# Attention kernel on one core: the product of probabilities and values over 512 queries at once, with five buffers for transposed heads

## What is computed

```
scores = jnp.einsum('bnhd,bmhd->bhnm', q, k) * scale        # 8 heads, HD = 32
scores = jnp.where(mask, jnp.float32(-jnp.inf), scores)
attn = jax.nn.softmax(scores, axis=-1)
h = jnp.einsum('bhnm,bmhd->bnhd', attn, v).reshape(b, n, d)  # the product of the change
h = h @ Wo + bo                                              # then residual and layer norm
```

## Time and profile before

| | |
|---|---|
| median of 3 runs | 1259.42 us (1255.37 to 1261.86) |
| span of the profiled execution | 1260.3 us, its own time; nothing is added around it in what follows |
| TensorE busy | 1175.5 us, 93% |
| VectorE busy | 1044.5 us, 83% |
| ScalarE busy | 881.5 us, 70% |
| one loop body | 73.88 us, 14 of them |
| granted TensorE clock, mean | 0.989 |

### The profile page before, as it was taken

The page is one execution under the profiler, slowest core; times in us unless marked ns, Lnnn a source line. Parts: engine busy times, 40 slices in busy tenths (PEclk is TensorE's granted clock), DMA queues, the critical chain, the costliest instruction groups (busy, mean ns, idle before and its releaser), DMA issues.

```text
span 1260.3 us, 28368 instructions
## 1 busy us (share of the span) xinstructions
PE 1175.5 (93%) x9440; PEld 846.5 (67%) x9440; DVE 1044.5 (83%) x2767; ACT 881.5 (70%) x2024; POOL 489.0 (39%) x337
## 2 busy tenths in 40 slices
PE   5877999999999999999999999999999999999896
PEld 2744767677776767767676776767677676767564
DVE  4775888889788888979889897988979798897686
ACT  3245786777777677777767777776777768677674
POOL 1360235433443443345334433633443363333320
PEclk9998999999999999999999999999999999999999
DMA  8125172543526153362624436153343615333321
GB/s 253 48 51 134 44 183 54 130 113 87 132 52 195 41 137 99 85 151 51 168 69 106 119 85 163 52 153 83 101 118 85 167 52 155 81 85 85 84 68 34
DMA packets 182208, 130.84 MB, mean 104 GB/s; under 512 B 108464, under 2 KB 161712, under 8 KB 182064
## 3 DMA queue, kind: packets, MB, share of 16 engines
q1 hardware_dynamic: 179904, 121.16, 37.4%
q0 software_dynamic: 2160, 7.87, 1.8%
HBM read 61.87 MB, written 25.17 MB: 69 GB/s over the span
## 4 chain that ended last, share of the span: by engine, by line
PE 51%; DVE 24%; issue 12%; ACT 10%; DMA 2%; POOL 0%; DVEq 0%; SPq 0%; ACTq 0%; POOLq 0%
PE ps_j L779 16%; PE ps_t L792 13%; PE ps_j L882 9%; DVE masked_s L1026 8%; ACT probs L933 5%; PE ps_s L771 4%; PE ps_j L899 4%; PE ps_s L765 3%; DVE y_l L1175 2%; ACT pt_h L939 2%; DVE parts L1183 2%; DVE pt_l L1061 2%; DVE stats_L L1046 2%; ACT xw L974 1%; ACT parts L982 1%
## 5 line engine op out<-in xcount | busy, mean ns | idle before, releaser
L933 ACT ACTIVATE probs<-masked_s,nm_h 128x512 f32<-128x512 f32 x512 | 367.6, 718 | 138.1 <-DVE nm_h L1026 136.9
L792 PE MATMUL ps_t<-ident,probs 128*128 128x128 f32 x2560 | 392.4, 276 | 36.5 <-ACT pt_h L939 19.7
L792 PEld LDWEIGHTS ps_t<-ident,probs 128*128 128x128 f32 x2560 | 302.9, 142 | 132.4 <-ACT probs L933 61.1
L1026 DVE CUSTOM_DVE_ANT_0 masked_s<-ps_s,mask_h 128x512 f32<-128x512 f32 x512 | 341.9, 681 | 58.6 <-PE ps_s L771 56.1
L939 ACT ACTIVATE pt_h<-ps_t 128x512 f32<-128x512 f32 x376 | 222.1, 591 | 97.2 <-PE ps_t L792 94.0
L771 PE MATMUL ps_s<-stack 128*128 128x512 f16 x512 | 195.0, 381 | 10.0 <-DVE nm_h L1026 6.4
L779 PE MATMUL ps_j<-xw,pt_l 128*128 128x256 f16 x1536 | 184.9, 275 | 0.0
L779 PEld LDWEIGHTS ps_j<-xw,pt_l 128*128 128x128 f16 x1536 | 151.4, 99 | 28.3 <-issue 0.5
L624 POOL TENSOR_TENSOR rstd_L<-var_eps_L,minus_half 128x4 f32<-128x4 f32 x32 | 32.8, 1024 | 299.3 <-DVE var_eps_L L1056 299.3
L882 PE MATMUL ps_j<-pt_h,v 128*32 128x256 f32 x2048 | 125.2, 386 | 1.7 <-DVE pt_h L1033 1.7
L624 POOL TENSOR_TENSOR rstd_F<-var_eps_F,minus_half 128x4 f32<-128x4 f32 x16 | 16.3, 1018 | 280.0 <-DVE var_eps_F L1056 280.0
(11 more groups left out here) (111 smaller groups left out, 1717.5 us busy)
## 6 DMA issues: line engine op xcount, KB each, us to landing
stack<-bounce SPq DMA_DIRECT2D x256, 128.0 KB, 3.1
bounce<-parts SPq DMA_DIRECT2D x64, 256.0 KB, 3.0
adj_t<-adj_dram SPq DMA_DIRECT2D x29, 512.0 KB, 4.9
x<-x_dram SPq DMA_DIRECT2D x16, 512.0 KB, 4.2
mask_a<-mask_a SPq DMA_DIRECT2D x16, 512.0 KB, 4.0
mask_h<-mask_a SPq DMA_DIRECT2D x64, 128.0 KB, 3.3
out_dram<-y_f POOLq DMA_DIRECT2D x15, 512.0 KB, 3.4
stack<-adj_dram SPq DMA_DIRECT2D x2, 512.0 KB, 6.4
```

The costliest lines, as they stand in the source:

```text
L792: last = pe.transpose(ps_t[r % 2][:, t], probs[:, r, t * P:(t + 1) * P], ident[:])
L933: act.activation(probs[:, r], masked_s[:, r], ACT.Exp, bias=nm[:, n, r:r + 1], scale=-1.0, accum_out=total[:, n, r:r + 1]).then_inc(exps, 1)
L1026: dve.tensor_tensor_reduce(out=masked_s[:, r], in0=ps_s[scores_bank(pos)][:], in1=m[:, r], scale=-scale, scalar=NONE_LEFT, op0=ALU.add, op ...
```

## The change

The product of a group goes in one part over all 512 queries in place of two parts over 256. It is still 16 matmuls, each with twice the columns. `OG` now has two parts (the product and the reciprocals); in the loop the product of group 0 moves from steps 3 and 5 to step 5, that of group 1 from steps 23 and 24 to step 25. The reciprocals stay at 7 and 26. Since the product comes after tiles 4 and 5 (24 and 25) are copied, `pt_h` becomes a ring of five buffers, indexed by head counted over all graphs. In the tail the three first groups change likewise; the very last keeps two halves under the name `OE`.

```diff
+PT_RING = 5
...
-    ("OG", (1, 0), "i", 0, (3, 5, 7)),
+    ("OG", (1, 0), "i", 0, (5, 7)),
...
-    ("OG", (1, 2), "i", 1, (23, 24, 26)),
+    ("OG", (1, 2), "i", 1, (25, 26)),
...
-    ("OG", (2, 0), "i", 0, (3, 4, 6)),
+    ("OG", (2, 0), "i", 0, (4, 6)),
...
-    ("OG", (0, 1), "i", 1, (19, 21, 24)),
+    ("OG", (0, 1), "i", 1, (20, 24)),
...
-    ("OG", (2, 0), "i+1", 0, (35, 37, 40)),
+    ("OG", (2, 0), "i+1", 0, (37, 39)),
...
-    ("OG", (1, 2), "i+1", 1, (51, 51, 51)),
+    ("OE", (1, 2), "i+1", 1, (51, 51, 51)),
...
-        pt_h = sb("pt_h", [P, 4, NT, N])
+        pt_h = sb("pt_h", [P, PT_RING, NT, N])
...
+        def pt_of(b, n):
+
+            return pt_h[:, (H * b + n) % PT_RING]
...
-                if name == "OG":
+                if name in ("OG", "OE"):
                     g, r = l, half
-                    if r < 2:
-
-                        for tile in range(2 * r, 2 * r + 2):
+                    pieces = 1 if name == "OG" else 2
+                    if r < pieces:
+
+                        tiles = range(NT // pieces * r, NT // pieces * (r + 1))
+                        at = slice(tiles[0] * P, (tiles[-1] + 1) * P)
+                        for tile in tiles:
                             pe.wait_ge(*copied(blk_.slot_of("H", 4 * g + 3, b), tile))
...
-                                last = pe.matmul(out_bank[h * HD:(h + 1) * HD, 2 * r * P:2 * (r + 1) * P],
-                                                 v1[:, t, col:col + HD], pt_h[:, h, t, 2 * r * P:2 * (r + 1) * P],
+                                last = pe.matmul(out_bank[h * HD:(h + 1) * HD, at],
+                                                 v1[:, t, col:col + HD], pt_of(b, 4 * g + h)[:, t, at],
                                                  start=t == 0, stop=t == NT - 1)
```

More of the change, by code:

```diff
@@ L98 @@
 PRO_TILES = NT * sum(len(slots) for _, slots, _, _ in PRO_BLOCKS)
-PARTS = {"AV": 4, "OG": 3, "R": 1, "N": 1, "S": 1, "B": 1, "D": 1, "M": 1}
+PARTS = {"AV": 4, "OG": 2, "OE": 3, "R": 1, "N": 1, "S": 1, "B": 1, "D": 1, "M": 1}
 DVE_TILES, LAST_DVE_TILES = (3,), (1, 3)
@@ L297, in copied, with products_done @@
             return copied_dve if by_dve(q, r) else copied_act, before + mine.index(r) + 1
+        def pt_of(b, n):
+            return pt_h[:, (H * b + n) % PT_RING]
+        def products_done(b, g):
+            return 2 * b + g + (2 if (b, g) == (NB - 1, 1) else 1)
         def scores_bank(pos):
@@ L392, in occupy @@
                     return before
-                side = half // 2 if name in ("AV", "OG") else half
+                side = half // 2 if name in ("AV", "OE") else half
                 before = self.in_bank.get(banks[side], ())
@@ L937, in copy_tile @@
                 act.wait_ge(transposed, NT * q + r + 1)
-                dst = (pt_l[:, 0] if kind == "L" else pt_h[:, n % 4])[:, :, r * P:(r + 1) * P]
+                dst = (pt_l[:, 0] if kind == "L" else pt_of(b, n))[:, :, r * P:(r + 1) * P]
                 act.activation(dst, ps_t[r % 2][:], ACT.Copy).then_inc(copied_act, 1)
@@ L983, in job @@
                         .then_inc(hi_ready["QK"[half]], 1)
-                if name == "OG" and half == 2:
+                if (name, half) in (("OG", 1), ("OE", 2)):
                     g = l
@@ L1190, in job @@
                         .then_inc(v_ready, 1)
-                if name == "OG" and half == 2:
+                if (name, half) in (("OG", 1), ("OE", 2)):
                     g = l
-                    dve.wait_ge(done["O"], 2 * (2 * b + g + 1))
+                    dve.wait_ge(done["O"], products_done(b, g))
                     dve.wait_ge(rb_ready, FIRST + 2 * b + g + 1)
```

## The result

The changed kernel takes 1278.08 us (median of 4 runs, 1274.28 to 1280.64), the kernel before 1258.05 beside it (4 runs). The ratio is 1.0158 with a 95% interval of 1.0137 to 1.0178: slower by about 20 us. The profiled execution has a span of 1276.0 us, 15.7 more than before.

A forecast was written before the change was run, and what follows sets the result against it. No single bound: TensorE busy 93% of the span, VectorE 83%, the chain crossing engines. Sum: 1260.3 + 7.4 (longer bodies) + 6.0 (clock falls) + 0 (tail) = 1273.7, as a median 1272.8; predicted 1273, range 1256 to 1283.

The forecast's parts named there:

- the new wait: TensorE before the transposes of tile 24: idle 1.27 us for the copy of tile 22.
- Group 0: Product merged in step 5: TensorE 0.28 us early, VectorE 0.36 us early on reaching the pinch.
- the pinch: Steps 22 and 23, where TensorE waits 0.40 and 1.03 us for VectorE and ScalarE.
- VectorE's gain in steps 5 and 6: VectorE's waits of 0.25 and 0.76 us for scores and the key half of QK largely go.
- The cap at tile 14: VectorE has at most 0.17 us of slack against TensorE at tile 14; 0.08 was taken.
- The saving of a merge: Merged product 3.59 us plus one pair of edges, 0.15: saves 0.28 us a group, between 0.15 and 0.41.
- The body: Each of 14 loop bodies 0.53 us longer, 74.4 us where no clock falls; 7.4 us in all.
- The clock: Behind the pinch, 5 falls in 14 bodies at 1.5 us each: 4 more than before, 6.0 us.
- The tail: Merged products after the loop cost 0 net, between -1.7 and +1.2 us.
- faster, if the pinch gave way: Transposes of tile 24 need no wait, both groups save, no new fall: 1251.6 us; chance 13%.
- About the same: Saving per group at its upper end, clock falls no oftener: 1263.2 us, or 1261.5; chance 20%.
- A fall in nearly every body: Clock falls in nearly every loop body: 25.4 us more, 1284.8 us; chance 12%.

The follow-up runs named there:

- group 0 alone: The kernel before with only group 0 of the loop merged, group 1 and the tail in halves: 1254.65 us, ratio 0.9971.
- the adjacent halves: The changed kernel with each loop product as two halves of 256 queries one right behind the other, at the same places: 1276.94 us, ratio 1.0179.
- The loop with the clock held up: Four extra matmuls per step: changed kernel, steps 22 and 23, 1267.97 us; kernel before with ring of five, step 22 only, 1258.62 us.

## Why the prediction was right

The forecast was 1273 (1256 to 1283) and slower; measured 1278.08. The mechanism was right: the new wait, where it stands, what sets it and how long it is. The number of falls rested on a misread row and came out near by luck.

- **Group 0.** Forecast 0.36 us early at the pinch; measured 0.37, both in the changed kernel and with group 0 alone. The way there was partly wrong. VectorE's gain in steps 5 and 6 was to be up to 1 us; the wait of 0.76 for the key half of QK only shrank to 0.61, and VectorE was 0.55 us early there and 0.41 up to tile 13. The cap at tile 14 took the last 0.04 (its low part starts 28.75 us into the body, 29.12 before). Nothing was run against the cap.
- **The saving of a merge.** Forecast 0.28 us for a group. Measured: 3.57 + 0.15 for the wide block against 4.02, so 0.30. The size was right and its reason wrong: I gave the 0.13 us to the instructions, and the adjacent halves show that it belongs to the block.
- **The new wait.** Forecast 1.27 us before transposes 24, set by the copy of tile 22 behind the late mask of tile 24. Measured 623.78 - 621.85 - 0.65 = 1.28. Moving one QH part away from that mask brought mask and transposes 0.66 us forward together and removed the loss, which shows the cause.
- **The body.** Forecast 74.41 us, measured 74.43; 14 x 0.55 = 7.7 us, forecast 7.4. The loop with the clock held up confirms it: 8.0.
- **The clock.** This is the term that was mis-sized. Forecast 5 falls at 1.5 us, 6.0 us net of the one before; measured falls in six bodies worth 9.9 us, net of the 1.7 before 8.2. A single fall cost 75.77 - 74.43 = 1.34 us, less than 1.5; but one slow stretch was twice as long as the others and came with a late mask (that body took 77.8 us), and neither was allowed for. The five falls themselves were a guess that came out well: they were argued from 1.43 us of idle time as the edge, since the body that fell had the same waits as the 13 others. It had not; it alone had a third wait of 0.19 us just before the fall. Nor were there 2.6 us of idle time after the change but, in brackets like those of the earlier trace rows, 0.34 + 1.03 + 1.03 = 2.40. Kernels with these waits, to within 0.06 us, had 4, 6 and 9 falls. With the late masks taken off both sides (0.8 and 0.2 us) the clock's own price is 7.6 us net. The Trainium skill's page "TensorE: Matmul & The Clock Gate", "A second HAM failure mode", which I had weighed against the single fall of before, is borne out in direction: repeated waits of 0.34, 1.03 and 1.03 us were enough in 6 of 14 bodies, and filling the two longer ones stopped the falls.
- **The tail.** Forecast 0, measured +0.3. The clock fell here all the same, but inside the merged product, which follows a wait of 3.00 us for the copy of tile 3 and took 5.3 us. The transfer behind it hides most of that: the QH job starts 19.7 us into the tail for 19.2 before, and now runs at full clock.
- In the profiled execution 8.0 + 8.2 + 0.3 - 0.8 (prologue) = 15.7, the whole difference. That the medians differ by 20 and not 15.7 is because of which executions were profiled: that of before took 1261.86 us in the metric, 3.8 above its median, and that of after 1277.70, 0.4 below. So of the 5 us between forecast and median 2.3 are errors of the sum (1276.0 for 1273.7 in the profiled executions), and 3 are this spread, which no term describes.

The rivals: faster, if the pinch gave way, fell with the measured wait of 1.28, above the 0.74 at which it would have turned. About the same: the lower end of the price was not met, and the clock fell more often. A fall in nearly every body: six of 14 here, but nine of 14 in the sibling with the product in step 24, so this rival wasn't far off.

## What to carry to other kernels

Before two pieces of filler work are merged into one, look at which waits they fill: a part that runs while another engine catches up hides that wait, and moved behind it, by as little as a step or two, it leaves the wait open and still costs its own length. Here the merge gained 0.37 us in the stretch where TensorE never stops and lost 0.91 right behind the place where it waits; doing only the first is 0.3% faster than the kernel before. Idle time of TensorE has a second price beside itself, the clock, and matmuls whose result nobody uses, put into a wait, can show how large it is. And before a row is called the same as its neighbours, compare every wait around it: the body with the fall had one more than the rest.

## What was not expected of the hardware

- Blocks of 128x32 matmuls with four heads side by side cost about 0.3 us for being a block (0.13 us beyond streaming, 0.10 before and 0.05 behind), at both lengths seen here: 64 instructions in a row took 3.59 us, 32 of double width 3.57, 32 of single width 1.86.
- Some slow stretches are twice as long, 6.8 us for 3.4. The one in the changed kernel, from 318.8 us on, made the body 3.37 us longer, 0.8 of it by the late mask. It had waits of 0.34, 1.03 and 0.70 us ahead of it, the last of which ends as it begins, and one of 0.81 inside:

```profile
318.87 0.61 PE L780 MATMUL ps_s<-stack 128*128 128x512 f16 x1 [0.70 <-DVE nm_h L1038]
320.29 1.09 PE L801 MATMUL ps_t<-ident,probs 128*128 128x128 f32 x4 [0.81 <-ACT pt_h L951]
```

- Extra matmuls on TensorE during the waits slowed neither ScalarE nor VectorE: their busy times in a body are 54.87 and 64.14 us with them, 54.89 and 64.14 without.
